# Decoder block on one core: self-attention recast as one interleaved pipeline of four groups, with moments taken early and four scatters abreast

## What is computed

```python
x = x + attn(layernorm(x), w_qkv, w_out)               # causal self-attention, no biases
x = x + xattn(layernorm(x), ctx, ctx, encoding, ...)   # rotary, scores over the 512 columns
x = x + moe(layernorm(x), Wg, W1, W3, W2, Ws1, Ws3, Ws2)
# attn: q, k, v = split(x @ w_qkv.T); softmax(causal(q @ k.T / sqrt(32))) @ v, then @ w_out.T
# moe: softmax router, top 2 of 4 groups, top 4 of 16 experts, two shared experts
```

## Time and profile before

| | us |
|---|---|
| median of three runs | 1920.51 |
| the profiled execution's own time | 1920.77 |
| its span | 1919.0 |
| self-attention, with its normalisation: 0 to 481.5 | 481.5 |
| cross-attention: 481.5 to 1133 | 651.5 |
| third normalisation, router, scatters: 1133 to 1334 | 201 |
| routed experts: 1334 to 1803 | 469 |
| gathers and second shared expert: 1803 to 1919 | 116 |

### The profile page before, as it was taken

One profiled execution on the slowest core, in us unless ns is written; L12 is line 12 of the kernel. 1 busy time (PEld: TensorE's weight loads), 2 busy tenths in 40 slices (PEclk: granted clock), 3 DMA queues, 4 the chain that ended last, 5 costly groups with the idle time before them and its releaser, 6 DMA issues. The chain is left out here.

```text
span 1919.0 us, 29165 instructions
## 1 busy us (share of the span) xinstructions
PE 1515.1 (79%) x9516; PEld 701.8 (37%) x9525; DVE 1094.0 (57%) x1809; ACT 625.1 (33%) x1103; POOL 681.2 (35%) x685
## 2 busy tenths in 40 slices
PE   1778787887157888888888847881899999999988
PEld 1334343434012222222222215340555555556443
DVE  6443444444557888888888547730354544444376
ACT  4312130303225656665666646110111111111121
POOL 3000000000445323323330021664464645676364
PEclk9989898898656898899999976995999999999999
DMA  4160708080346211211211012143666657563465
GB/s 175 49 204 26 227 0 252 0 251 1 101 105 176 53 42 39 56 40 39 56 38 19 1 48 94 61 170 131 186 177 162 164 144 176 157 203 88 118 188 182
DMA packets 183543, 211.00 MB, mean 110 GB/s; under 512 B 89968, under 2 KB 135600, under 8 KB 182960
## 3 DMA queue, kind: packets, MB, share of 16 engines
q1 hardware_dynamic: 154224, 123.73, 24.0%
q0 software_dynamic: 18592, 66.99, 11.4%
q10 hardware_dynamic: 10656, 19.40, 2.6%
HBM read 101.09 MB, written 88.87 MB: 99 GB/s over the span
## 5 line engine op out<-in xcount | busy, mean ns | idle before, releaser
L804 DVE TENSOR_REDUCE ca_mx<-ca_sc 128x1 f32<-128x512 f32 x512 | 327.6, 678 | 93.7 <-PE ca_sc L724 93.4
L77 PE MATMUL re_ab<-fx_w,re_xt 128*128 x1800 | 296.6, 315 | 52.3 <-DMA re_xt<-slot_rows 52.2
L937 ACT ACTIVATE ca_pt<-ca_st 128x512 f32<-128x512 f32 x512 | 264.7, 596 | 106.7 <-PE ca_st L736 106.7
L724 PE MATMUL ca_sc<-ca_ks,ca_qs 48*128 48x512 f16 x512 | 191.6, 428 | 54.3 <-DVE ca_mx L804 29.8
L77 PEld LDWEIGHTS re_ab<-fx_w,re_xt 128*128 128x128 f16 x1800 | 173.6, 98 | 150.7 <-issue 54.7
L736 PE MATMUL ca_st<-ca_qs,ca_ks 49*128 49x512 f16 x512 | 173.1, 402 | 40.9 <-ACT ca_pt L937 35.2
L77 PE MATMUL re_yp<-fx_w,re_ht 128*128 (+1 forms) x666 | 156.0, 379 | 0.0
L478 POOL TENSOR_TENSOR sa_yt<-sa_yf,sa_yt 128x512 f16<-128x512 f32 x16 | 18.5, 1158 | 385.4 <-ACT sa_yt L461 385.4
L1492 POOL TENSOR_TENSOR fx_w<-re_raw_w,fx_w 128x272 f16<-128x272 f32 x224 | 154.2, 725 | 1.7
L749 PE MATMUL ca_pv<-ca_pt,ca_va 128*32 128x512 f32 x1024 | 150.0, 650 | 1.0 <-DVE ca_turned L817 0.5
L77 PE MATMUL sh_ab<-fx_xn,sh_pair 128*128 (+3 forms) x576 | 129.7, 388 | 3.8 <-PEq L1420 3.3
(11 more groups left out here) (236 smaller groups left out, 2437.0 us busy)
## 6 DMA issues: line engine op xcount, KB each, us to landing
re_raw_w<-in_we POOLq DMA_DIRECT2D x56, 544.0 KB, 4.7
slot_rows<-sa_zeros SPq DMA_DIRECT2D x12, 1792.0 KB, 16.1
slot_outs<-re_ys ACTq DMA_DIRECT2D x74, 256.0 KB, 2.0
sa_scratch<-sa_qk SPq DMA_DIRECT2D x16, 512.0 KB, 4.8
ca_scratch<-ca_qk SPq DMA_DIRECT2D x64, 128.0 KB, 1.8
sa_qs<-sa_scratch SPq DMA_DIRECT2D x12, 512.0 KB, 7.1
sa_ks<-sa_scratch SPq DMA_DIRECT2D x12, 512.0 KB, 7.0
ca_qs<-ca_scratch SPq DMA_DIRECT2D x48, 128.0 KB, 3.7
```

The costliest lines, as they stand in the source:

```text
L77: last = nc.tensor.matmul(out, lhs(a, c), rhs(b, c), start=(c == 0 and n == 0), stop=(c == chunks - 1 and n == len(PRODUCTS) - 1))
L724: nc.tensor.matmul(sc[:, m % RING, :], qs[rows, c % SLOTS, pair, qt * P:(qt + 1) * P], ks[rows, c % SLOTS, pair, :], start=True, stop=True ...
L804: nc.vector.reduce_max(mx[:, qd // 4, qd % 4, 2 * a + jj:2 * a + jj + 1], sc[:, m % RING, :], AX.X).then_inc(maxed, 1)
L937: nc.scalar.activation(pt[:, (4 * qd + k) % 8, :], st[:, m % RING, :], ACT.Exp, scale=SCALE).then_inc(exp_done, 1)
```

## The change

`layer_norm` is now used only for the feed-forward part. It works in quarters of four tiles (add epsilon, root, inversion, then the tiles), keeps its pairs in `rows` itself, and finds the moments of tiles 0 to 13 already there. Those are taken in cross-attention, two tiles in each of seven steps of the last batch; cross-attention's own moments are taken inside self-attention (`measure_rows`). `row_moments` becomes `row_scale`, with the root alone. The first shared expert's weights come in four pieces. `ABREAST` is 4.

Self-attention has no block ahead of it and no loop: a function `walk` gives one order, which TensorE, VectorE and ScalarE each follow with their own parts. `qs` and `ks` have two slots. The raw weights lie in `qs` until it is first loaded. GpSimd subtracts weight chunks 0 and 1, VectorE chunks 2 and 3; GpSimd then makes the masks and fills the row of ones in both slots of `ks`, two memsets of 1 x 8192, and last subtracts the output weights.

```diff
+        def walk(normalise, low_part, turn, qk_unit, v_unit, out_unit, measure_rows, score, negate, maxima, attend):
+            for k in range(DC):
+                normalise(1, k)
+                qk_unit(0, 2 * k)
+                low_part(1, k)
+                qk_unit(0, 2 * k + 1)
+                turn(1, k)
+            for g in range(NG):
+                units = [(v_unit, g, t) for t in range(4)]
+                if g:
+                    units += [(out_unit, g - 1, t) for t in range(4)]
+                if g + 1 < NG:
+                    units += [(qk_unit, g + 1, u) for u in range(2 * DC)]
+                def slot(i):
+                    if i < len(units):
+                        make, of, k = units[i]
+                        make(of, k)
+                        if g and i == 9 or g + 1 == NG and i == 7:
+                            measure_rows(g - 1)
+                        for j in range(4 if g + 2 < NG else 0):
+                            if i == 3 * j + 1:
+                                normalise(g + 2, j)
+                            if i == 3 * j + 2:
+                                low_part(g + 2, j)
+                            if i == min(3 * j + 3, 11):
+                                turn(g + 2, j)
+                for n in range(SCORES):
+                    score(g, n)
+                    if n == SCORES - 1:
+                        negate(g)
+                    if n % 2:
+                        slot(n // 2)
+                slot(SCORES // 2)
+                maxima(g)
+                for i in range(SCORES // 2 + 1, len(units)):
+                    slot(i)
+                attend(g)
+            for t in range(4):
+                out_unit(NG - 1, t)
+            measure_rows(NG - 1)
...
+            def v_unit(g, t):
+                if g and t < 2:
+                    pe.wait_ge(norm_done, 4 * g)
...
+                ends = sc[:, n % 4, :].rearrange("p (h k) -> p h k", h=heads)[:, :, keys - P:keys]
+                nc.tensor.matmul(ends, identb[:, :], mask[:, 0:heads, :], start=False, stop=True,
+                                 skip_group_check=True).then_inc(score_done, 1)
...
+                    last = nc.tensor.matmul(st.rearrange("p (a c) -> p a c", a=3)[:, 0:3:2, :], identb[:, :],
+                                            maskt[:, :, :], start=False, stop=True, skip_group_check=True)
...
+            for q in range(1, NG):
+                measure(q, own, True)
+            deviate(4, NT)
+            invert(4, NT, 2)
+            walk(normalise, low_part, skip, qk_unit, v_unit, out_unit, measure_rows, score, negate, skip, attend)
...
+            for s in range(2):
+                nc.gpsimd.memset(ks[PB:PR, s, :, :], 1.0).then_inc(made, 1)
+                pool.wait_ge(made, 9 + s)
...
+            load_rows(0)
+            for c in range(DC):
+                sp.dma_start(raw[:, c, :], wqkv_dram.rearrange("(c p) e -> p c e", p=P)[:, c]).then_inc(w_loaded[c], 16)
+            for q in range(1, 4):
+                load_rows(q)
...
+            zero = lambda rows, z: sp.dma_start(
+                rows.rearrange("(p a) (b n) -> p (a b) n", p=P, b=2),
+                z.rearrange("p (o n) -> p o n", o=1).to_broadcast([P, rows.shape[0] // P * 2, z.shape[1]])
+            ).then_inc(cleared, 16)
...
+        cuts = (0, EW // 2, EW, (EW + WC) // 2, WC) if turn == 0 else (0, EW, WC)
...
-ABREAST = 2
+ABREAST = 4
```

More of the change, by code:

```diff
@@ L79, in split_product, with layer_norm @@
     return last
-def layer_norm(nc, name, x_sb, xn, ident, rows=None, source=None, before=lambda block: None, after=lambda block: None):
+def layer_norm(nc, name, x_sb, xn, ident, rows, before, moments, measured):
     with ExitStack() as ctx:
@@ new lines, in released, with take @@
+            def released(n):
+                kind, g, k = users[n]
+                if kind == "turn":
+                    pe.wait_ge(xn_kept, 4 * g + k + 1)
+                elif kind == "qk":
+                    pe.wait_ge(qk_low, 2 * DC * g + k + 1)
+                elif kind == "v":
+                    pe.wait_ge(v_kept, 4 * g + k + 1)
+                else:
+                    pe.wait_ge(out_added, 4 * g + k + 1)
+            def take(*user):
+                if place[user] >= 2:
+                    released(place[user] - 2)
+                return bank(*user)
@@ L398, in _ @@
                         if p < PAIRS:
[L399 to L403 removed]
+                            transposed_scores(g, p)
+                    values(g, qd)
+            for j in range(4):
+                turn(0, j)
+            walk(skip, skip, turn, qk_unit, v_unit, out_unit, skip, score, skip, maxima, attend)
@@ L468, in _ @@
                                          ACT.Exp, scale=SCALE).then_inc(exp_done, 1)
                     if p % 4 == 3 and p > 3:
-                        high(p // 4 - 1)
-                high(3)
+                        y_high_part(g, p // 4 - 1)
+                y_high_part(g, 3)
+            root(0, 4, 1)
+            high_part(0, 0)
+            high_part(0, 1)
+            for j in range(4):
+                weights(j)
+                keep(0, j)
+                if j + 2 < 4:
+                    high_part(0, j + 2)
@@ L473, in _ @@
+            root(4, NT, 2)
+            weights(DC)
+            walk(high_part, skip, keep, qk_unit, skip, skip, skip, skip, skip, maxima, attend)
         @block.gpsimd
         def _(pool):
-            with pool.Fori(0, T // G) as g:
-                for hq in range(4):
-                    pool.wait_ge(y_high, 4 * g + hq + 1)
-                    nc.gpsimd.tensor_tensor(yt[:, 1, hq, :], yf[:, hq % 2, :], yt[:, 0, hq, :],
-                                            ALU.subtract).then_inc(y_low, 1)
@@ L1694, in decoder_block @@
         x_sb = sb("x_sb", [P, NT, D], F32)
+        moments = sb("moments", [P, NT, 2], F32)
         ident = sb("ident", [P, P], F16)
```

591 lines of the change are left out of this document (341 added, 250 removed).

## The result

The changed kernel takes 1873.25 us in the median of four runs (1865.69 to 1878.36), against 1919.08 before (four runs): ratio 0.9758, 95% interval 0.972 to 0.9797. It is faster, but 39 us behind the 1834 that I forecast, and 5 us above the top of the range. The profiled execution took 1878.36 us, its span is 1876.6. One plain remark for what follows: two profiled executions can differ by several us in stretches where the kernels are alike. The kernel before and a variant of it (experiment 2) run the same instructions up to the first scatter and reached it at 1229.0 and 1221.7 us. Differences of stages are therefore good to a few us.

What follows compares the result with a forecast made beforehand. TensorE's idle time in self-attention (481.5 of 1919 us) and its 47.88 us wait for scatters bound the kernel. Self-attention -68.8, third normalisation -2.5, scatters -15.5: -86.8 from the profiled 1920.77, giving 1834 us; range 1812 to 1868.

Steps and rivals of the forecast that it cites:

- Start of self-attention: Self-attention's loads to first scores: first product at 25.3 in place of 69.47 us, scores at 88.2, not 111.04.
- second start: Self-attention's start: after two units TensorE waits until 46 us, with VectorE held behind GpSimd's memsets until 41.
- last low part: Self-attention's start: the low part after TensorE's last starting units, forecast at 70.6 us; the copies follow.
- copies: Self-attention's copies through DRAM: 17.55 us before scores; late copies rival, twice that and scores waiting, 1868 us, chance 0.06.
- quick start rival: Self-attention's start: VectorE passes GpSimd's memsets, seven us less, 1827 us; chance 0.15.
- The four groups: Self-attention's groups: attentions end at 161.2, 243.6, 321.8, 390.3 us, stage at 412.7 in place of 481.5, minus 68.8.
- Units and maxima: Self-attention slots: VectorE's 1.9 us hidden under TensorE's 3.3; rival, units and evictions in step, 1933 us, chance 0.04.
- Moments and third normalisation: Cross-attention's moments cost zero; the normalisation ahead of the router gains 2.5 us, between -5 and +1.
- Scatters: Scatters after the router: 1.29 us a step for 1.54, minus 15.5 us; rival, pace kept, 1849 us, chance 0.10.

Runs made afterwards that it cites:

- experiment 2: Kernel before the change, with four scatters in flight in place of two, all else as before: 1942.62 us, ratio 1.012.
- experiment 8: Changed kernel with two scatters in flight and GpSimd's two long memsets replaced by 128 x 64 ones sent by DMA: 1834.64 us, ratio 0.9584.
- experiment 1: Changed kernel with two scatters in flight in place of four, all else as changed: 1837.44 us, ratio 0.9567.
- experiment 7: Changed kernel with two scatters in flight for the first 26 scatters, then four: 1838.48 us, ratio 0.9594.
- 13: Changed kernel, four scatters in flight, with 200 one-column ScalarE copies written out beside the scatters: 1877.07 us, single execution with the added work.
- 14: Changed kernel, four scatters in flight, with 200 one-column ScalarE copies as a loop of one copy: 1924.75 us, single execution with the added work.

## Why the prediction was wrong

- **Start of self-attention: right in mechanism, 6.5 us too slow at its end.** The forecast stands in brackets: first product 26.75 (25.3), VectorE behind the memsets to 38.5 (41; a memset took 6.95, not 7.6), second start 46 (46), end of the last low part 67.6 (70.6), copies 14.0 us (17.55), scores 81.7 (88.2). The quick start rival is refuted, and experiment 8 shows that it would have been worth 3.5 us, not 7.
- **The four groups: right.** The attentions ended at 156.2, 241.2, 319.4 and 388.0 (161.2, 243.6, 321.8, 390.3), the last moments at 411.4 (412.7). Units and maxima did lie beside each other, the copies were late for no group but the first. Minus 70.1 for minus 68.8: the lead of 6.5 us at the first scores had shrunk to 1.3 at the end, so the groups and the end took 5 us more than forecast, and part of the good fit is luck.
- **Moments and third normalisation: right within the spread.** Cross-attention 649.1 us for 651.5; from its end to the router's first product 41.2 for 43.7, minus 2.5 as forecast. The first scatter came at 1151.0, 78.0 us earlier where the terms give 71.3; 3.1 of the difference lie between the router's first product and the first scatter, which I had held unchanged.
- **Scatters: the step that failed.** "I take 1.29 ... **Minus 15.5**; the ends are 0 (the queue gives 1.54 whatever is in flight) and 17.4." The step was right, 1.284; its cover was not looked at. I priced the scatters alone, as the end of their stage, and held TensorE's shared work beside them to be free, since it had waited 47.88 us for them. Both my bounds were gains; a loss was not among them, nor among the rivals, though no row excluded it. At 100 rows a us that work stretches from 61 us after the first scatter (experiment 1) to 132, past the scatters, and sets the end: plus 27.6 in place of minus 15.5. Experiment 1 takes this one term out and lands at 1837.44; there the forecast without it is 1849.5, which is 12 too high; in that run's profile 11 of them lie ahead of the scatters (the first comes 82.4 us earlier than before, for 71.3).
- **The rest.** From the first routed product to the end the changed kernel's profile shows 8 us more than before. The same stretch took between 577.5 and 588.2 us in the experiments, with 588.7 in the changed kernel, and the highest and the lowest compute the same there; so I put this down to spread. The terms add up: 43.1 for the scatters, less 6.7 ahead of them, and 8.0 here are 44.4, from 1834 to the profiled 1878.36.

What stays open is which part of the chip is short. Shown is: ScalarE's issues fall to one in 1.40 us and TensorE's to one in about that, with instructions used before held as well; VectorE and ScalarE also took up finished work tens of us late in some runs (in experiment 2, ScalarE took up at 1275.11 a product that was finished at 1243.8). With four in flight from the start it sets in 16 to 25 us after the first scatter, with four after 26 at the slower pace (experiment 7) after 10 us, and it lasts until 7 to 9 us after the start of the last scatter (the changed kernel, 13 and 14). That looks like something that fills up and drains, but no run shows what. It goes with the rows written out a us: TensorE is held at 94 and at 100, free at 52 and from 82 to 85. It does not go with bytes, the profile's packets, the number of scatters in flight, TensorE's loop or GpSimd's load. What sets the bound, which lies between 85 and 94 rows a us, was not tried. Nor was the nearest rival for the cause: every execution here was recorded by the profiler, and no run shows whether one without its records is held in the same way.

## What to carry to other kernels

Before a transfer or a queue is made faster, ask what runs beside it, and put the loss of that cover among the bounds: a faster background job can cost the foreground more than it saves (27.6 us lost here where 15.5 were to be won). Where GpSimd writes out rows at such a pace, keep a pause between its scatters while other engines have work, and take the pause away when they are done; read the windows of every engine beside it, for a hold shows as idle "issue" with nothing waited for. And keep long memsets of one partition off GpSimd at the moment when VectorE is on the critical path; here that was worth about 3 us.

## What the runs showed of the hardware that I had not expected

- Beside scatters of 128 rows every 1.28 us ScalarE issued a copy every 1.40 us, where with a scatter every 1.51 us it took 0.09; TensorE did 7 products in 20 us in place of 95, and its granted clock fell to 0.50 (1.2 GHz) while it crept.
- 64 rows every 1.24 us did nothing of the kind, at about the bytes a us of 128 rows of half the length, which did.
- A memset of 8192 columns on a single partition took GpSimd 6.95 us, and a VectorE TENSOR_SCALAR of 12 numbers that began beside it lasted until it ended, 3.68 us in place of 0.17.
